# Attention maxima with key rows masked per head: two heads share the products of both layers

## The reference

```
# layer 0: windows of 64, a query sees the 64 keys before it and itself
scores = jnp.einsum('bhnid,bhnjd->bhnij', qc, kc) * scale
band = (j >= i) & (j <= i + C)
scores = jnp.where(mask[None, None], scores, jnp.finfo(scores.dtype).min)
probs = jax.nn.softmax(scores, axis=-1)
# layer 1: one key and one value head for all 16 query heads, strictly causal
scores = jnp.einsum('bhtd,bsd->bhts', q, k) * scale
mask = pos[None, :] < pos[:, None]
scores = jnp.where(mask[None, None, :, :], scores, NEG_BIG)
attn = jax.nn.softmax(scores, axis=-1)
```

## Time and profile before

| what | us |
|---|---|
| median of three runs | 645.83 |
| the three runs | 645.83, 641.29, 645.98 |
| the profiled execution | 641.25 |
| its span, first to last instruction | 639.4 |
| mean granted TensorE clock, share of full speed | 0.99 |

### The profile page before, as it was taken

How to read it: one execution, slowest core, us unless ns; L and a number is a source line. 1 busy time by engine, 2 the same in 40 slices (tenths; PEclk the granted TensorE clock), 3 DMA queues, 4 the chain that set the end, 5 groups by cost and what they waited for, 6 DMA issues and landing times.

```text
span 639.4 us, 10621 instructions
## 1 busy us (share of the span) xinstructions
PE 593.7 (93%) x3880; PEld 463.8 (73%) x3890; DVE 372.0 (58%) x709; ACT 302.4 (47%) x466; POOL 117.9 (18%) x90
## 2 busy tenths in 40 slices
PE   4898899898999999999998897789999999999995
PEld 4788545686888888888886675443447788888885
DVE  6478646754434455444557699794376533344556
ACT  3667665564333333333433572458764643333331
POOL 4500021223112222222130000002201231222220
PEclk9999979999999999999999899999999999999999
DMA  8464664000111111111100034302210000111101
GB/s 322 126 225 141 233 189 141 2 14 12 31 46 49 49 49 41 37 45 49 49 26 1 0 101 116 121 27 84 87 38 2 26 25 26 50 49 49 49 1 66
DMA packets 22194, 44.65 MB, mean 70 GB/s; under 512 B 3632, under 2 KB 7632, under 8 KB 22160
## 3 DMA queue, kind: packets, MB, share of 16 engines
q1 hardware_dynamic: 21840, 44.05, 21.5%
q10 hardware_dynamic: 320, 0.13, 0.1%
HBM read 33.16 MB, written 11.01 MB: 69 GB/s over the span
## 4 chain that ended last, share of the span: by engine, by line
PE 71%; DVE 18%; ACT 5%; issue 2%; DMA 2%; POOL 1%; ACTq 0%; SPq 0%; DVEq 0%
PE PS L553 32%; PE PS L997 15%; DVE nmx L1587 5%; PE PS L880 4%; PE PS L849 2%; PE PS L714 2%; PE PS L828 2%; PE PS L712 2%; PE PS L833 2%; DVE stats L1481 1%; PE PS L726 1%; DVE x L1656 1%; DMA qk_slot<-rows_scr 1%; PE PS L895 1%; PE PS L591 1%
## 5 line engine op out<-in xcount | busy, mean ns | idle before, releaser
L1320 ACT ACTIVATE qk_hi<-xn 128x512 fp32r<-128x512 f32 x82 | 51.7, 631 | 166.6 <-DVE xn L1801 137.0
L553 PE MATMUL PS<-h_hi,wqkv_hi 128*128 128x512 f32 x304 | 103.0, 396 | 3.0 <-DVE h_lo L1515 2.3
L553 PE MATMUL PS<-h_hi,wqkv_lo 128*128 128x512 f32 x272 | 92.4, 396 | 1.8 <-DVE xn L1711 1.8
L1798 DVE TENSOR_TENSOR prs<-prs,PS 128x512 f32<-128x512 f32 x60 | 41.2, 687 | 84.6 <-PE PS L553 84.6
L519 POOL TENSOR_TENSOR wqkv_hi<-fw_raw,wqkv_hi 128x768 fp32r<-128x768 f32 x18 | 33.1, 1839 | 248.5 <-ACT wqkv_hi L1296 248.5
L1805 DVE TENSOR_TENSOR qk_lo<-xn,qk_hi 128x512 fp32r<-128x512 f32 x70 | 48.5, 693 | 50.3 <-ACT qk_hi L1320 50.3
L1316 ACT ACTIVATE prs<-PS 128x512 f32<-128x512 f32 x82 | 48.7, 594 | 49.5 <-PE PS L553 49.5
L553 PEld LDWEIGHTS PS<-h_hi,wqkv_hi 128*128 128x128 f32 x304 | 57.2, 188 | 15.3 <-DVE h_lo L1515 2.9
L553 PE MATMUL PS<-h_lo,wqkv_hi 128*128 128x512 f32 x160 | 62.9, 393 | 0.0
L553 PEld LDWEIGHTS PS<-h_hi,wqkv_lo 128*128 128x128 f32 x272 | 51.1, 188 | 13.3 <-DVE xn L1711 2.7
L1587 DVE TENSOR_REDUCE nmx<-PS 128x1024 f32 (+4 forms) x48 | 50.8, 1128 | 5.6 <-PE PS L731 5.6
(11 more groups left out here) (259 smaller groups left out, 1182.3 us busy)
## 6 DMA issues: line engine op xcount, KB each, us to landing
fw_raw<-in_ffn SPq DMA_DIRECT2D x41, 384.0 KB, 3.1
qk_slot<-rows_scr SPq DMA_DIRECT2D x32, 200.0 KB
rows_scr<-qk_hi SPq DMA_DIRECT2D x16, 256.0 KB
qk_slot<-q_scr SPq DMA_DIRECT2D x32, 100.0 KB
rows_scr<-qk_lo SPq DMA_DIRECT2D x8, 256.0 KB
wmod<-in_wmod SPq DMA_DIRECT2D x1, 1536.0 KB, 13.0
x<-in_x SPq DMA_DIRECT2D x2, 512.0 KB, 4.3
wmod<-in_wmod SPq DMA_DIRECT2D x1, 1024.0 KB, 9.3
```

Of the source, the lines that this page charges most:

```text
L553: ins = nc.tensor.matmul(dst, left(a, c), right(b, c), start=n == 0, stop=n == total - 1)
L1320: nc.scalar.activation(hidR[b][0], hid[b], ACT.Copy).then_inc(f["hi"], 1)
L1798: tt(hid[buf] if half is None else gu[buf], gact[buf], PS[:, 5, :], ALU.mult).then_inc(f["gu"], 1)
```

## The change

In both layers the keys are masked per head in place of the queries, the raw query tile is the stationary operand, and the masked keys of two heads lie side by side as one moving operand. One product so gives two heads. The core of the diff:

```diff
-WIDTH1 = [2 * P, 2 * P, 3 * P, 4 * P]
-BANK1 = [(0, 0), (0, 2 * P), (1, 0), (2, 0)]
+PIECES1 = [(0, 1, P), (1, 1, 2 * P), (2, 2, 3 * P), (4, 2, 4 * P)]
+def heads1(j):
+    return j % 4 // 2, 2 * (j // 4) + j % 2
...
                 if l == 0:
-                    k = qkR[0][:, bass.ds(2 + (g - BQ * b) // 2, 1), :].rearrange("p m t -> p (m t)")
+                    if s % 2 == 0:
+                        return
+                    n = 2 * g + s // 2
+                    q = qkR[0][:, (g - BQ * b) // 2, :]
+                    k = q_masked[:, (s - 1) * S:(s + 1) * S].rearrange("p (h k) -> p h k", h=2)
                     for t in range(NT):
-                        bank, col = 2 * (s % 2) + t // 2, (t % 2) * KEYS0
                         if t % 2 == 0:
-                            ge(a["mxd"], 2 * (u - 2) + t // 2 + 1)
-                            nc.tensor.matmul(PS[:, bank, 0:2 * KEYS0], identB[:, :], mask0[t // 2], start=True, stop=True)
+                            ge(a["mxd"], 2 * (n - 1) + t // 2 + 1)
+                            for i in range(2):
+                                nc.tensor.matmul(PS[:, t + i, 0:2 * KEYS0].rearrange("p (h k) -> p h k", h=2), identB[:, :],
+                                                 mask0[t + i > 0], start=True, stop=True)
                         before = WIN * (t > 0)
-                        ins = nc.tensor.matmul(PS[:, bank, col + WIN - before:col + KEYS0], qm[s][:, t * P:(t + 1) * P],
-                                               k[:, t * P - before:(t + 1) * P], start=False, stop=True,
+                        of = PS[:, t, 0:2 * KEYS0].rearrange("p (h k) -> p h k", h=2)
+                        ins = nc.tensor.matmul(of[:, :, WIN - before:KEYS0], q[:, t * P:(t + 1) * P],
+                                               k[:, :, t * P - before:(t + 1) * P], start=False, stop=True,
...
+            def scores1(b, j):
+                a = at[1]
+                n = b * H // 2 + j
+                m, p = heads1(j)
+                pe.wait_ge(a["qm"], b * H // 2 + 2 * p + 2)
+                k = q_masked[:, 2 * (p % 2) * S:2 * (p % 2 + 1) * S].rearrange("p (h k) -> p h k", h=2)
+                for qt, (bank, banks, w) in enumerate(PIECES1):
+                    q = q1R[b][0][:, m, qt * P:(qt + 1) * P]
+                    ge(a["mxd"], NT * (n - 1) + qt + 1)
+                    if banks == 1:
+                        of = PS[:, bank, 0:2 * w].rearrange("p (h k) -> p h k", h=2)
+                        nc.tensor.matmul(of, q, k[:, :, 0:w], start=True, stop=True, skip_group_check=True)
+                        ins = nc.tensor.matmul(of[:, :, w - P:w], identB[:, :], mask1[:, 0:P].unsqueeze(1).to_broadcast([P, 2, P]),
+                                               start=False, stop=True, skip_group_check=True)
+                    else:
+                        for h in range(2):
+                            nc.tensor.matmul(PS[:, bank + h, 0:w], q, k[:, h, 0:w], start=True, stop=True, skip_group_check=True)
+                        for h in range(2):
+                            ins = nc.tensor.matmul(PS[:, bank + h, w - P:w], identB[:, :], mask1[:, 0:P], start=False, stop=True,
+                                                   skip_group_check=True)
                     ins.then_inc(a["s"], 1)
...
-                later = {1: (0, 1), 3: (1, 2), 5: (1, 0), 7: (1, 1), 9: (1, 3)}
+                later = {0: (0, 1), 1: (1, 2), 2: (1, 0), 3: (1, 1), 4: (1, 3)}
...
-                ge(a["s"], 3 * (2 * g + s // 2 - 1) if l else 2 * (u - 3))
+                ge(a["s"], (2, 3)[l] * (2 * g + s // 2 - 1))
...
+            def mask_k1(b, i):
+                p = 4 * b + i // 2
+                ge(at[1]["s"], NT * (4 * (p // 2 - 1) + 3 + p % 2))
+                nc.scalar.activation(qm[2 * (p % 2) + i % 2][:, :], q1R[b][0][:, 2, :].bitcast(F32), ACT.Copy,
+                                     scale=headmask[:, i:i + 1]).then_inc(at[1]["qm"], 1)
...
+                if l == 0:
+                    for i in range(2):
+                        ge(a["s"], 2 * n + i + 1)
+                        nc.vector.tensor_reduce(of.rearrange("p h t -> p t h")[:, 2 * i:2 * i + 2, :],
+                                                PS[:, 2 * i:2 * i + 2, 0:2 * KEYS0].rearrange("p t (h k) -> p t h k", k=KEYS0),
+                                                X, ALU.max, negate=True).then_inc(a["mxd"], 1)
+            def maxima1(b, j):
...
+                for qt, (bank, banks, w) in enumerate(PIECES1):
+                    ge(a["s"], NT * n + qt + 1)
+                    if banks == 1:
+                        scores = PS[:, bank, 0:2 * w].rearrange("p (h k) -> p h k", h=2)
+                    else:
+                        scores = PS[:, bank:bank + 2, 0:w]
+                    nc.vector.tensor_reduce(of[:, :, qt], scores, X, ALU.max, negate=True).then_inc(a["mxd"], 1)
```

More of the change, by code:

```diff
@@ L97, in build @@
         maskB = sb("maskB", [P, 5 * KEYS0 + 3 * P], BF16)
-        mask0 = [maskB[:, 0:2 * KEYS0], maskB[:, KEYS0:3 * KEYS0]]
+        mask0 = [maskB[:, i * KEYS0:(i + 1) * KEYS0].unsqueeze(1).to_broadcast([P, 2, KEYS0]) for i in range(2)]
         mask0T = maskB[:, 3 * KEYS0:5 * KEYS0]
@@ L734, in scores @@
-                for piece, tiles in enumerate(((0, 1), (2,), (3,))):
-                    ge(a["mxd"], 3 * (n - 1) + piece + 1)
-                    for h in range(2):
-                        for qt in tiles:
-                            products(qt, h)
-                    for h in range(2):
-                        for qt in tiles:
-                            ins = masked(qt, h)
+            def scores1(b, j):
[18 more added lines that the diff above has]
+                                                   skip_group_check=True)
@@ L1448, in _ @@
             max_high(1, 0)
-            mask_rest(1, 1)
+            for i in range(4, H // 2):
+                mask_k1(1, i)
             exp_table()
@@ L1573, in maxima @@
                 h = s % 2
-                if l == 0:
-                    for i in range(2):
-                        ge(a["s"], 2 * u + i + 1)
-                        nc.vector.tensor_reduce(nmx[:, bass.ds(NT * u + 2 * i, 2)],
-                                                PS[:, 2 * h + i, 0:2 * KEYS0].rearrange("p (t k) -> p t k", k=KEYS0),
-                                                X, ALU.max, negate=True).then_inc(a["mxd"], 1)
-                    return
                 if s % 2 == 0:
@@ L1883, in _ @@
             q1_low(0, 0)
-            later = {2: lambda: h_low(2, 1), 6: lambda: q1_low(0, 1), 8: lambda: q1_low(1, 2), 10: lambda: q1_low(1, 0),
-                     12: lambda: q1_low(1, 1), 13: lambda: take_v1(1)}
-            for i in range(H):
-                maxima(1, i // SLOTS, i % SLOTS)
-                if i in later:
-                    later[i]()
-            maxima_first(1, 1)
+            later = {0: lambda: h_low(2, 1), 2: lambda: q1_low(0, 1), 3: lambda: q1_low(1, 2), 4: lambda: q1_low(1, 0),
+                     5: lambda: q1_low(1, 1), 6: lambda: take_v1(1)}
+            for j in range(H // 2):
+                maxima1(0, j)
+                if j in later:
+                    later[j]()
+            maxima1(1, 0)
+            maxima1(1, 1)
             max_low(1, 0)
-            maxima_rest(1, 1)
+            for j in range(2, H // 2):
+                maxima1(1, j)
             max_low(1, 1)
```

84 lines of the change are left out of this document (37 added, 47 removed).

## The result

The changed kernel took 639.06 us in the median of nine runs (637.14 to 640.02); the kernel before, with six further runs beside it, 643.9 (641.29 to 646.5). The ratio is 0.9925, with an interval of 0.9903 to 0.9946: 4.8 us faster (3.5 to 6.2), or 0.5 to 1.0%, less than the 1% that counts as a change here. The forecast was 0.57%, 3.65 us. The profiled execution of the changed kernel took 639.43, with a span of 637.6.

What follows compares the result with a forecast made beforehand. It took VectorE's reductions to bound layer 1's maxima, with VectorE and TensorE nearly matched in layer 0's. From 641.25 us, 5.8 less for layer 1 and 2.1 more for layer 0 gave 637.6, range 633.5 to 645.

Steps and rivals of the forecast that it cites:

- Layer 1, -5.8: Layer 1's maxima: 0.5 from the first piece, 3.0 from reductions and 2.3 from idle places, 5.8 us earlier.
- The price line: VectorE reductions cost 1.03 ns an element plus 0.077 us an instruction; a layer 1 pair takes 2.94 us, 0.19 less.
- the idle places behind the first reduction: VectorE in layer 1: idle places of 0.42, 1.52 and 2.55 us become one of 2.0; 2.3 kept.
- The first piece: Start of layer 1's maxima: one product and one mask, ready after about 0.5 us against 1.21; 0.5 gained.
- rival three: Layer 1's gain shrinks by 3 of the 5.8 through costlier small reductions or a stalled handover: 640.6 us, chance 0.13.
- Layer 0, +2.1: Layer 0's maxima and the load behind them make the kernel 2.1 us later, bounds 0 and 3.7.
- 2.0 for the pair: Layer 0 loop: with two pieces in flight a pair takes 2.0 us against 1.89, bounds 1.74 and 2.2.
- ends 1.7 late: Layer 0's first loop: six pairs at 2.0 with four gate steps end 1.7 us late, and ScalarE's release with them.
- batch-1 loop 2.0 late: Layer 0, batch 1: one mask more ahead of the loop, partly covered by projections, makes it 2.0 us late.
- 2.0 to 2.1: Slot 0's second load, behind layer 0's maxima: it lands 2.0 to 2.1 us later, not 2.5.
- Rivals one and two: One: drop at 80 to 88 us avoided, 634.8, chance 0.25; two: 1.2 GHz inside layer 0's maxima, 646.0, chance 0.12.
- Rival four: Layer 0 pairs: products written into two runs take 0.11 us more, 1.7 in all: 639.3 us, chance 0.05.

Runs made afterwards that it cites:

- after: The changed kernel's own profile: both layers' parts of the change against the kernel before; median 639.06 us, ratio 0.9925.
- l1_only_b: Repeat of layer 1's part of the change alone, layer 0 as in the kernel before; 636.77 us, ratio 0.986.
- l1_fill: Layer 1's part alone, plus eight unread 512-column products ahead of TensorE's wait for slot 0's second load; 635.89 us, ratio 0.984.
- l1_fill_shift: Layer 1's part alone, plus unread products ahead of slot 0's load wait and of each four 2-column matmuls; 635.58 us, ratio 0.986.
- before_b: The kernel before, profiled once more with no edit; 642.24 us in one run.
- l0_only: The kernel before with layer 0's maxima alone changed (keys masked, two-bank pieces, a ring of two); 645.97 us, ratio 1.0053.
- after_fill: The changed kernel with one unread 512-column product ahead of each pair of batch 0's layer 0 loop; 638.65 us, ratio 0.991.
- l0_ring4: The changed kernel with layer 0's pieces cut to one bank each, four in flight; 637.88 us, ratio 0.990.
- after_shift: The changed kernel with one 512-column product ahead of each four 2-column matmuls between layer 0's batches; 637.18 us, ratio 0.988.
- before: The kernel before, without the change, in its first profile; median 643.9 us.
- l1_only: The changed kernel with layer 0's maxima put back as in the kernel before; 637.28 us, ratio 0.990.

## Why the prediction was right

**Layer 1, -5.8: right, and by its own terms.** The price line held at both sizes that no row had shown. Six pairs behind the change of batch take 17.62 in place of 18.86, 0.21 a pair where 0.19 was said; the idle places behind the first reduction went from 4.5 to 2.0, for which 2.3 was kept. So the stage is 5.74 shorter where these two terms made 5.3, and all eight profiles with the new order, whatever their layer 0, lie between 53.10 and 53.13. The first piece was there after 0.63 in place of 1.21. In the two profiles first compared that gain cannot be seen, since the third drop was longer in the profile after. Where that drop was as long as in the profile after, the first reduction comes 28.2 to 28.5 behind layer 1's normalisation with the new layer 1 (after, l1_only_b, l1_fill, l1_fill_shift) and 28.9 and 29.2 with the old (before_b, l0_only); where it was as short as before, 27.0 to 27.4 against 27.9. So it is 0.6 to 0.7 sooner on average, for the 0.5 that was said. No reduction waited on TensorE in mid-batch, so rival three is out.

**What layer 1 gave beyond that.** The measured 4.8 is 1.2 more than the 3.65 of the sum, which lies inside the interval of 3.5 to 6.2, so the 1.2 need not be anything. The profiles do offer a reason. In the old order the clock fell at the change of batch in three of four profiles (before_b, layer 0's part alone, the old order of pairs), and the stage with the old code then took 60.3 in place of 58.84. In the new order it did not fall there in any of eight. A drop worth 1.5 in two of three profiles with the old layer 1 is 1.0 on average, close to the 1.2. The granted clock of the other runs points the same way: over the whole span it was 0.984 or less in 33 of the 53 runs of the kernel before that stand beside the experiments, as in before_b (0.984), and 0.988 to 0.996 in all nine of the changed kernel; where the clock fell in them is not on record. That the shorter wait of the new order is what keeps the clock up is not shown: no run changed that wait alone.

**Layer 0, +2.1: near in sum, two terms too small.** 2.0 for the pair was 2.03, the wait for V and the two masks ahead of the loop made its start 1.08 late (39.91 less 1.59, against 37.24) where 1.1 was said, and the wait for the load was 0.98 for 0.9. Too small was "ends 1.7 late": ScalarE's release came 2.4 late (52.29 less 1.59, against 48.31). Of the missing 0.7, 0.44 is the pause of 0.64 ahead of the loop's second pair, where 0.2 was expected; the chain puts it down to issue on VectorE, and no run looked further. It stands in every profile with this loop (0.63 or 0.64 in four, 0.73 in after_fill), so it is no chance of one execution. Too small as well was "batch-1 loop 2.0 late": it was 4.4 late (63.75 less 1.59, against 57.75). The drop right behind batch 0 is 1.5 of that (the same loop starts at 59.3 in before_b and l1_only_b), so 2.9 belong to the change. 2.4 come with ScalarE's release; and TensorE stands 2.04 ahead of the loop in place of 1.27, since one more mask comes first. The prediction let 0.3 of that mask through behind the projections; 0.5 came through. ScalarE's timeline shows the release:

```profile
52.29 1.15 ACT L1228 ACTIVATE qk_hi<-hF 128x512 fp32r<-128x512 f32 x2 [2.27 <-PE PS L725]
```

Of the 5.1 at the key-major scores about 1.5 belongs to the drop (71.5 against 69.94 in the kernels with the old layer 0) and 3.6 to the change, where 2.5 was said. The landing gave 1.1 of that back: 2.5 late like for like, where "2.0 to 2.1" was said. The load went out 3.5 later, where the prediction had 2.0. So the sum is near because the load took less time in the kernels that issued it later, which made up for most of the two terms that were too small; the prediction had allowed for 0.4 of this, and why the load takes less is not shown.

**Where it was luck.** Like for like, layer 1 gives 6.4 and layer 0 takes 2.5, so 3.9 in all for the 3.65 of the sum. The single profile shows only 1.8: its start is 1.6 late, the longer third drop takes the first piece's gain and 0.5 more, and the drops in and behind layer 0's maxima stand elsewhere than before and give 0.7 back. None of that was in the sum, so where in the stated range the time fell is in part luck.

**Rivals one and two.** The profile after seems to show both, and neither holds as a reason. A granted clock under 1.00 before 72 us did come, which the prediction had named as what would make it wrong; but it lasted for some 3 us and not for twelve pairs, and the kernel before has it too. The drop at 80 to 88 did stay away, but not because the wait shrank, since the old layer 0 waited 1.66 and 1.90 there at full clock. In the table each profile has one drop or none, here or there; comparing one profile with the drop at 80 with one that has it at 52 shows a gain of 2.8 that the drop's place makes. Whether the change makes the one place likelier is not shown: of the profiles without added products the drop is at 80 in two of four with the old layer 0 and in none of three with the new (l0_ring4 aside). Rival four is out. From start to start the products of a pair's first piece, 640 columns and in two runs in part, take 0.43, and the 768 columns of the second piece take 0.49 (31.17 to 31.60 and 31.80 to 32.29); with 0.11 more for the two runs the first would have been the slower.

```profile
31.17 0.59 PE L725 MATMUL PS<-q_masked,qk_hi 128*128 128x256 f32 x2
31.60 0.50 PE L721 MATMUL PS<-maskB,identB 128*128 128x384 bf16 x2
31.80 0.65 PE L725 MATMUL PS<-q_masked,qk_hi 128*128 128x384 f32 x2
32.29 0.40 PE L559 MATMUL PS<-h_hi,wqkv_hi 128*128 128x512 f32 x1
```

The masks of layer 1's first two pieces (L744, 256 columns, in one run and in two) took 0.28 in all 32 cases.

## What to carry to other kernels

A reduction's price line from two sizes held at four, so cutting a stage to fewer elements can be costed ahead; but merging two pieces into one halves the pieces in flight, and a pair of reductions that is 8% cheaper by the price line (1.74 for 1.89) took 7% longer in the ring (2.03). Order the work so that what is behind a handover needs nothing that is made behind it: that was worth 1.5 to 2.4 us here, against some 3 from the smaller reductions. Before one reads a gain or a loss out of a clock drop in a single profile, take a second profile of the same kernel.

## What the runs showed of the hardware that was not expected

TensorE's drop to 1.2 GHz is not tied to one place of a program. The kernel before had it at 80 to 88 us behind a wait of 1.43 in one execution, and at 48 to 56 behind 16 matmuls of 2 columns in the next. Of the ten profiles without products among those matmuls eight have a drop between 48 and 60 us, of the two with them neither; in the changed kernel the drop then came at 64 to 68, in the kernel with the old layer 0 and both sets of products not at all until 356. Two profiles make that likely and no more. The drop ahead of layer 1's stage stands in all twelve, short or long as in the two profiles shown.

The granted clock column does not show every slow stretch. In 18 to 21 us of the profile after it says 1.00, but products of 512 columns start 0.43 apart (18.22, 18.65, 19.07), and 0.23 apart from 21.15 on; in the profile before they start 0.23 apart from 17.94 on. 0.43 is 512 columns at 1.2 GHz. Eight of the twelve profiles begin so, with the old and with the new layer 0, the kernel before in neither of its two; in seven of the eight V's projections come 1.4 to 2.1 us late by it, in the eighth 3.5, since the work ahead was late as well. It belongs to no part of the change. The Trainium skill (TensorE: Matmul & The Clock Gate, Part 1: The HAM clock gate) says that the same kernel meets the change of clock after a different number of matmuls from run to run; these profiles agree, 7 slow products in l1_fill_shift and 10 in after_shift, and show it for the drops further on too.

The load of slot 0, issued at 71.40 and 72.41 in kernels with the same layer 0 (before and l1_only), was used after 8.5 and 9.7 us; nothing in these runs says why.
